# Attention and out-projection in one program per layer: a two-layer gated cross-attention kernel on one core

## What is computed

```
x = x + tanh(g_xattn[0]) * attn0(layernorm(x), ctx)   # 32 heads, 8 kv heads, 128 features, q and k rms-normed
x = x + tanh(g_ffn[0])   * scaled_ffn(layernorm(x))
x = x + tanh(g_xattn[1]) * attn1(layernorm(x), ctx)   # 16 heads, 4 kv heads, 96 features
x = x + tanh(g_ffn[1])   * routed_lora(layernorm(x))

attn(latents, context):                # 8 batches, 112 latent rows, 375 context rows, 1024 features
    kv = concat(context, latents)      # 487 rows
    q, k, v = latents @ Wq, kv @ Wk, kv @ Wv
    out = softmax(q k^T * scale) v     # 4 heads share one kv head
    return out @ Wo
```

## Time and profile before

| | us |
|---|---|
| median of 3 runs | 3026.83 (3024.57 to 3027.17) |
| span of the profiled execution | 3023.0 |
| PE busy, share | 2842.8, 94% |
| PEld busy, share | 2421.8, 80% |
| ACT busy, share | 1214.6, 40% |
| DVE busy, share | 1164.5, 39% |
| POOL busy, share | 710.5, 24% |

### The profile page before, as it was taken

The page is one execution under the profiler, slowest core; times in us unless marked ns, Lnnn a source line. Parts: engine busy times, 40 slices in busy tenths (PEclk is TensorE's granted clock), DMA queues, the critical chain, the costliest instruction groups (busy, mean ns, idle before and its releaser), DMA issues. The chain is left out here.

```text
span 3023.0 us, 43041 instructions
## 1 busy us (share of the span) xinstructions
PE 2842.8 (94%) x14487; PEld 2421.8 (80%) x14487; DVE 1164.5 (39%) x2034; ACT 1214.6 (40%) x2550; POOL 710.5 (24%) x585
## 2 busy tenths in 40 slices
PE   6999999799999997999998999598998998998997
PEld 5888887688888886888886888477998997887885
DVE  4333330411112116777772332643101112776335
ACT  4333332322222216777772323434322223785223
POOL 1111110300000005666655732120000001553400
PEclk9999999899999998999998999798998999999998
DMA  4233333222221213333336721102241222332312
GB/s 143 77 101 101 100 102 112 100 63 68 67 61 61 62 55 110 106 106 106 107 88 158 179 65 55 66 1 79 82 117 56 92 92 79 81 83 71 87 34 63
DMA packets 331149, 259.89 MB, mean 86 GB/s; under 512 B 190160, under 2 KB 285768, under 8 KB 331056
## 3 DMA queue, kind: packets, MB, share of 16 engines
q1 hardware_dynamic: 331056, 258.63, 29.3%
HBM read 190.66 MB, written 67.91 MB: 86 GB/s over the span
## 5 line engine op out<-in xcount | busy, mean ns | idle before, releaser
L42 PE MATMUL kv_y<-kv_whi,kv_xthi 128*125 128x512 f32 (+1 forms) x1152 | 446.0, 387 | 4.6 <-DVE kv_wlo L295 4.2
L44 PE MATMUL kv_y<-kv_whi,kv_xtlo 128*125 128x512 f32 (+1 forms) x1152 | 434.7, 377 | 0.0
L43 PE MATMUL kv_y<-kv_wlo,kv_xthi 128*125 128x512 f32 (+1 forms) x1152 | 433.9, 377 | 0.0
L42 PE MATMUL q_y<-q_whi,xthi 128*128 128x512 f32 (+1 forms) x1008 | 386.3, 383 | 8.0 <-ACT q_qn L487 4.7
L44 PE MATMUL q_y<-q_whi,xtlo 128*128 128x512 f32 (+1 forms) x1008 | 376.7, 374 | 0.0
L43 PE MATMUL q_y<-q_wlo,xthi 128*128 128x512 f32 (+1 forms) x1008 | 376.2, 373 | 0.0
L1000 DVE TENSOR_TENSOR at_ptlo<-at_tb,at_pthi 125x448 fp32r<-125x448 f32 (+1 forms) x384 | 238.2, 620 | 143.8 <-ACT at_pthi L953 137.9
L42 PE MATMUL o_y<-o_whi,o_ohi 128*128 128x512 f32 (+1 forms) x672 | 267.3, 398 | 14.4 <-DVE o_olo L1163 12.1
L953 ACT ACTIVATE at_pthi<-at_tb 125x448 fp32r<-125x448 f32 (+1 forms) x384 | 210.1, 547 | 136.2 <-PE at_tb L909 131.9
L43 PE MATMUL o_y<-o_wlo,o_ohi 128*128 128x512 f32 (+1 forms) x672 | 263.9, 393 | 0.0
L44 PE MATMUL o_y<-o_whi,o_olo 128*128 128x512 f32 (+1 forms) x672 | 263.8, 393 | 0.0
(11 more groups left out here) (192 smaller groups left out, 4819.9 us busy)
## 6 DMA issues: line engine op xcount, KB each, us to landing
kv_xin<-in_ctx_dram SPq DMA_DIRECT2D x48, 500.0 KB
q_raw<-in_L_xattn_Wq_dram SPq DMA_DIRECT2D x8, 2048.0 KB, 8.5
o_raw<-in_L_xattn_Wo_dram SPq DMA_DIRECT2D x64, 256.0 KB, 2.6
qT_d<-q_stage SPq DMA_DIRECT2D x56, 256.0 KB, 2.6
at_qr<-qT_d SPq DMA_DIRECT2D x64, 224.0 KB, 3.2
o_rb<-rT_d SPq DMA_DIRECT2D x32, 448.0 KB
v_d<-kv_stage SPq DMA_DIRECT2D x48, 250.0 KB
kT_d<-kv_stage SPq DMA_DIRECT2D x48, 250.0 KB, 4.5
```

What stands on the lines that cost most here:

```text
L42: pe.matmul(out, stat_hi, mov_hi, start=start, stop=False)
L43: pe.matmul(out, stat_hi, mov_lo, start=False, stop=False)
L44: return pe.matmul(out, stat_lo, mov_hi, start=False, stop=stop)
```

## The change

`attention`, `out_project` and the old `attend` are replaced by one `attend`. It is straight-line code: Python loops over all units, no hardware loop.

- Units now run kv head by kv head (a group g of 8 batches; `u = g * 8 + b`), and the projection of group g-1 is woven into the units of group g. A piece is one row tile of 128 tokens by 512 columns over the 4 heads of a group: 4 blocks of 128 features in layer 0 (12 matmuls), 3 in layer 1 (9 matmuls). There are 14 per group; a unit has an early piece (behind T1, not in batch 0) and a late one (behind V1, not in batch 7). All pieces use one PSUM bank `y`, and DVE adds each to the residual (`add`) before the next begins. The last group's 14 pieces come at the end, over four banks. The scores have three banks in place of four.
- The row sums' reciprocals are stored and fetched per unit: `spread_sums(u)` writes the 112 x 4 tile transposed to DRAM (runs of one element), `fetch_sums(u)` reads it back for all partitions. On SP both stand in one queue with the loads: sums of u stored, q, k, v of u+2 loaded, a slab of Wo loaded, sums of u fetched. `load(u+2)` has the same five DMAs as before.
- DVE normalizes each unit out of PSUM (`take_o`); ACT and POOL cut it into `oh` and `ol`. `oT` is gone.
- In layer 1 the four heads of 96 features are packed into three blocks of 128: block j holds head j and 32 features of head 3. Wo's slabs are loaded in the same order by two DMAs, turned on PE into `y`, and cut by ACT and DVE. 24 slabs take the place of 32; in layer 0 there are 64 as before, cut by ACT and POOL.
- The rows of x for the residual are loaded at the start of the stage.

```diff
@@ -96,7 +96,7 @@
-                      dram(f"rT{n}_d", (BATCH, L.heads, QLEN)))
+                      dram(f"rT{n}_d", (L.units, G, QLEN)))
...
+        def attend(n, L, x_sb, wo, source=None):
...
+            D, U, NB = L.d, L.units, BATCH
...
+            flip = not L.normed
+            NG = L.kvh
+            NK = G * D // P
+            NS = 2 * NK
...
+            def slab_step(m):
+                half, j = m // NK, m % NK
+                return half * 4 + j if not flip else m if half == 0 else 4 + j
...
+            def early_of(u):
+                g, k = u // NB, u % NB
+                return PIECES * (g - 1) + 2 * k - 1 if g and k else None
+            def late_of(u):
+                g, k = u // NB, u % NB
+                return PIECES * (g - 1) + 2 * k if g and k < NB - 1 else None
...
+            def piece(q):
+                g, i = q // PIECES, q % PIECES
+                if g < NG - 1:
+                    return g, i // TT, i % TT
+                return g, i % 2, i // 2
...
+                rb = sb(st, f"{tag}_rb", [D, 2, G, QLEN])
+                on = sb(st, f"{tag}_on", [P, 2, NK, QLEN]) if flip else rb
+                oh = sb(st, f"{tag}_oh", [P, 2, NK, TOKENS], F32R)
...
+                raw = sb(st, f"{tag}_raw", [P, RAW, BANK])
+                w_hi = sb(st, f"{tag}_whi", [P, 3, NK, BANK], F32R)
...
+                s = [ps(st, f"{tag}_s{i}", [P, BANK]) for i in range(3)]
...
+                y = ps(st, f"{tag}_y", [P, BANK])
+                tail_banks = [y] + s
...
+                        def load(u):
+                            g, b, p = u // NB, u % NB, u % 2
+                            if u >= 2:
+                                sp.wait_ge(q_cut, u - 1)
+                                sp.wait_ge(k_cut, u - 1)
+                            sp.dma_start(qr[:, p, :].rearrange("d (g s) -> d g s", g=G),
+                                         qT_d[g, :, :, b * QLEN:(b + 1) * QLEN]).then_inc(qk_loaded[p], 16)
+                            sp.dma_start(kr[:, p, 0:CTX], kT_d[b * L.kvh + g, :, :]).then_inc(qk_loaded[p], 16)
+                            sp.dma_start(kr[:, p, CTX:KVLEN], kl_d[g, :, b * QLEN:(b + 1) * QLEN]).then_inc(qk_loaded[p], 16)
+                            if u >= 2:
+                                sp.wait_ge(v_cut, u - 1)
...
+                            sp.dma_start(vr[0:CR, p, 0:CT, :], v_d[b * CTX:(b + 1) * CTX, cols].rearrange("(j r) d -> r j d", r=CR)).then_inc(v_loaded[p], 16)
+                            sp.dma_start(vr[0:QLEN, p, CT, :], vl_d[b * QLEN:(b + 1) * QLEN, cols]).then_inc(v_loaded[p], 16)
...
+                        def spread_sums(u):
+                            sp.wait_ge(inverted, u + 1)
+                            sp.dma_start(rT_d[u].rearrange("h s -> s h"), rinv[:, u % 2, :], allow_slow_non_contiguous=True).then_inc(r_stored[u % 2], 16)
+                        def fetch_sums(u):
+                            sp.wait_ge(r_stored[u % 2], 16 * (u // 2) + 16)
+                            if u >= 2:
+                                sp.wait_ge(o_taken if flip else o_lo, u - 1)
+                            sp.dma_start(rb[:, u % 2, :, :], rT_d[u:u + 1].broadcast_to([D, G, QLEN])).then_inc(r_loaded[u % 2], 16)
...
+                        load(0)
+                        load(1)
+                        if source is not None:
+                            for t in range(TT):
+                                sp.dma_start(x_sb[:, t, :], source[t * P:(t + 1) * P, :]).then_inc(x_loaded, 16)
...
+                        for w in range(RAW):
+                            load_slab(w)
...
+                        for u in range(U):
+                            spread_sums(u)
+                            if u + 2 < U:
+                                load(u + 2)
+                            if u % NB in SLAB_AT and slabs < NG * NS:
+                                load_slab(slabs)
...
+                            fetch_sums(u)
...
+                        def cut_o(u):
+                            g, b, p = u // NB, u % NB, u % 2
...
+                            pool.wait_ge(o_hi, u + 1)
+                            pool.tensor_tensor(ol[:, g % 2, :, cols], on[:, p, :, :], f32(oh[:, g % 2, :, cols]), ALU.subtract).then_inc(o_lo, 1)
...
+                        def project_piece(q, bank):
+                            g, half, t = piece(q)
+                            i = 2 * g + half
+                            pe.wait_ge(w_lo_s, NK * (i + 1))
+                            pe.wait_ge(o_lo, units_for(g, t))
+                            for k in range(NK):
+                                last = product(pe, bank[:], oh[:, g % 2, k, t * P:(t + 1) * P], ol[:, g % 2, k, t * P:(t + 1) * P],
+                                               w_hi[:, i % 3, k, :], w_lo[:, i % 3, k, :], k == 0, k == NK - 1)
+                            last.then_inc(projected, 1)
+                        def project_early(u):
+                            q = early_of(u)
+                            if q is not None:
+                                pe.wait_ge(added, q)
+                                if flip:
+                                    pe.wait_ge(w_lo_s, slabs_by(u))
+                                project_piece(q, y)
+                        def project_late(u):
+                            q = late_of(u)
+                            if q is not None:
+                                if q:
+                                    pe.wait_ge(added, q)
+                                if flip:
+                                    pe.wait_ge(w_lo_s, slabs_by(u + 1))
+                                project_piece(q, y)
+                        def turn_slab(u):
+                            if flip and u % NB in SLAB_AT:
+                                w = slabs_by(u)
+                                done = pieces_by(u) + (early_of(u) is not None)
+                                if done:
+                                    pe.wait_ge(added, done)
+                                if w:
+                                    pe.wait_ge(w_lo_s, w)
+                                pe.wait_ge(raw_loaded[w % RAW], 32 * (w // RAW) + 32)
+                                for m in range(G):
+                                    last = pe.transpose(y[:, m * P:(m + 1) * P], raw[:, w % RAW, m * P:(m + 1) * P], ident[:])
+                                last.then_inc(w_turned, 1)
...
+                            scores(0, h)
+                        for u in range(U):
+                            more = u + 1 < U
+                            if more:
+                                scores(u + 1, 0)
+                            turn(u, 0)
+                            if more:
+                                scores(u + 1, 1)
+                            turn(u, 1)
+                            project_early(u)
+                            if more:
+                                scores(u + 1, 2)
+                            if u:
+                                multiply(u - 1, 2)
+                            turn(u, 2)
+                            turn_slab(u)
+                            if more:
+                                scores(u + 1, 3)
+                            if u:
+                                multiply(u - 1, 3)
+                            multiply(u, 0)
+                            turn(u, 3)
+                            multiply(u, 1)
+                            project_late(u)
+                        multiply(U - 1, 2)
+                        multiply(U - 1, 3)
+                        first = PIECES * (NG - 1)
+                        for i in range(PIECES):
+                            pe.wait_ge(added, max(first, first + i - 3))
+                            project_piece(first + i, tail_banks[i % 4])
...
+                        def cut_o(u):
+                            g, b, p = u // NB, u % NB, u % 2
+                            act.wait_ge(o_taken, u + 1)
+                            if g >= 2 and b == 0:
+                                act.wait_ge(projected, PIECES * (g - 1))
+                            act.activation(oh[:, g % 2, :, b * QLEN:(b + 1) * QLEN], on[:, p, :, :], ACT.Copy).then_inc(o_hi, 1)
...
+                            high(u, 0)
+                            if u + 2 < U:
+                                cut_q(u + 2)
+                            high(u, 1)
+                            if more:
+                                exp(u + 1, 0)
+                                exp(u + 1, 1)
+                            high(u, 2)
+                            if u % NB in SLAB_AT:
+                                cut_slab(slabs_by(u))
+                            if more:
+                                exp(u + 1, 2)
+                            if u:
+                                cut_o(u - 1)
+                            high(u, 3)
+                            if more:
+                                exp(u + 1, 3)
```

(71 more changed lines are left out.)

489 lines of the change are left out of this document (158 added, 331 removed).

## The result

| | before | after |
|---|---|---|
| median of the runs, us | 3026.8 | 4163.8 (4152.6 to 4171.2, 4 runs) |
| ratio after / before, 95% interval | | 1.3756 (1.3734 to 1.3778) |
| span of the profiled run, us | 3023.0 | 4169.4 |
| PE busy, us | 2842.8 | 3047.5 |
| layer 0, first score to end of last add | 1150.7 to 1915.6 | 1145.8 to 2766.9 |

The changed kernel is 37.6% slower. I had forecast 8% slower, 3268 us, with a range up to 3461. The sign was right; the size was not, and the time lies far above the range. Layer 0 ends 851 us later (forecast 161), and layer 1 adds 295 (forecast 80).

The account below looks back on a forecast made before the run. The prediction took TensorE's own pace to bound the kernel, with a load wait of 5.4 us added per unit. Span 3023 + 161 (layer 0) + 80 (layer 1) = 3264, plus 3.8 for the median: 3268 us, range 3110 to 3461.

Parts of the forecast that it names:

- The place: SP's queue: load(u+2) stands behind the store of u's sums, so its full latency falls between two DVE instructions.
- the 8.75 us chain: Layer 0 unit with both pieces: from the load's landing through cuts, PE work, late piece and add to the next reciprocal, 8.75 us.
- the 12.24 worked out: PE's own work in a layer 0 unit with two pieces: 6.80 + 24 x 0.2267 = 12.24 us.
- the store at nothing: The 4-byte row-sum store ahead of the loads: nothing added for the middle, up to 2 us for the upper bound.
- L: Load latency between DVE's reciprocal and cut_k, in all but two units per layer: 5.4 us, range 3.7 to 7.5.
- Rival (c): The 4-byte store holds the queue longer, each run 0.2 us or more: L of 9 us, 3600 us; chance 0.07.
- The clock: PE's clock falls to half in each unit's gap: +230 us in 70 units with a late piece, 3500 us; chance 0.10.
- The savings: Two stage boundaries, about 30 us, and layer 1's packing, 38 us: 68 us earlier if PE stays the pace.
- The prediction's 2955: Whole kernel if PE stays the pace: ends at 2955 us; with the load hidden, 2959, a rival with chance 0.06.
- chain of 7.0 us for a unit without pieces: First 8 units of layer 0, without pieces: the chain over DVE and ACT ends by 7.0 us, against 6.80 of PE work.
- the 38 us of the packing: Layer 1's projection: packing 16 heads into 12 blocks cuts 672 matmuls to 504, 168 x 0.2267 = 38 us saved.
- the 30 of the boundaries: PE's loss between attention and projection, 13.4 + 2.5 us in layer 0 and 11.6 + 2.5 in layer 1, about 30 saved.

Follow-up runs that it names:

- experiment 1: Changed kernel with the store of the row sums left out, the fetch reading x instead (sums not applied): 3429.5 us.
- experiment 9: Changed kernel with 16-byte store runs, q and k loaded one unit further ahead, the slab's load one unit later: 3009.2 us, 0.9948 of the kernel before.
- experiment 4: Changed kernel with the same 448 4-byte runs each written 512 bytes from the next, the fetch reading x (sums not applied): 3434.6 us.
- experiments 3: Changed kernel storing the sums of two of four heads, 224 runs of 4 bytes, the fetch reading x (sums not applied): 4066.2 us.

## Why the prediction was wrong in size and right in kind

**The place, the chain, the sign: right.** In the kernel after, the reciprocal, the store, the load and the cuts follow each other as described, and the 8.75 us chain was measured at 8.78 to 8.80 in all 14 units of experiment 1 in which the granted clock stayed at 1.00. With the loads moved out of it, PE took over the pace: a steady unit with two pieces in experiment 9 is 12.3 us, against the 12.24 worked out.

**The term that failed: the store at nothing.** I took L = 0.25 + 0.45 + 4.7 and for the 4-byte store up to 2 us more, by the store of the earlier trace rows. That row was the nearest by kind but not by what counts: its runs are 448 bytes long, so no two of its writes come near each other except at their ends. Here 112 writes lie in each 448 bytes. The store lands after 10.3 us at the median, and L is 13.4 us. Without the store it is 6.2, so the store is 7.2 us of L, and 666 us over the 92 units. Experiment 1 against the kernel after gives 734, the clock's share with it. The step from "no row so short" to "small runs as such need not cost much" was true (experiment 4) and yet no bound for this store. Rival (c) had the sign, loads that land after 6 us and more (11.1 here), and a price of 0.2 us a run, which experiments 3 and 4 refute. Its total, L of 9, was still too small, and 0.07 too little chance for a kind of transfer that no row showed.

The prediction set a rule of the Trainium skill beside this (DMA: Bandwidth & Descriptors, Specifications: below 512 bytes a transfer is a read-modify-write). By size alone, wherever the writes lie, the kernel of experiment 4 should have been as slow, and it was not; the measurement decides. That a load needs longer when a slow store is in front of it agrees with another section of the Trainium skill (DMA: Bandwidth & Descriptors, Queues, rings and completion order), by which the receipt of a transfer lands only after all earlier writes of the same DMA engine: 11.1 us for the kl load here, 3.1 in experiment 4.

**The rest of L: one value for two layers.** Without the store L is 7.2 us in layer 0 and 4.0 in layer 1, where the sum had 5.4 for both: 73 us too little over the 92 units. The earlier trace rows had shown 5.87 and 3.80 from the q load's issue to the cut; I took 4.7, and experiment 1 has 5.4 and 3.9. The wake and the store's issue were put at 0.7. In layer 0 the head of the queue takes 1.85 in experiment 1, with no store to issue: the slab's load, waiting for POOL, and the fetch stand in front of the next unit's q load, 2.7 us in the unit shown. I had listed what waits behind the new wait on DVE, ACT and PE, and for SP only the store.

**The clock: a rival that came on top.** I gave 0.10 to a fall in every gap, as a case of its own at L = 5.4. It isn't one of its own: it comes with L. In the kernel after, the gaps are about 10 us and T2 to the late piece takes 6.25 instead of 3.34, 2.9 us in the unit shown; its chain from 1713.89 to 1725.49 is 11.60. The whole excess can be added up from the trace. Over the 92 units the waits sum to 1236 us where 92 x 5.4 = 497 had been forecast, 739 more. The chains sum to 959 us where the prediction's add up to 788, 171 more. The two make 910, and the span is 905 us above the forecast 3264. Of the 171, 102 are in the 48 units of layer 0 with a late piece: 10.92 us each, against 8.79 at a clock of 1.00. The other 69 are in the units without one and in layer 1, where the clock was not told from other causes. In experiment 1 the same sums are 73 and 99. So the store costs 666 us by itself and 72 more through longer chains. The cases of my range were added one at a time, while the first of them brings the second with it.

**The savings: real, but smaller than 68 us.** The prediction's 2955 for a kernel at PE's pace is tested by experiment 9, where DVE waits for a load six times, 46.5 us in all, 43.3 of it before the first unit of each layer. It has a span of 3007.7. Layer 0's last add ends there at 1917.7 (before 1915.6), layer 1's at 2937.0 (2953.4): 16 us, not 68. In layer 0 the eight units without pieces take 69.4 us by the distances of their reciprocals where 8 x 6.80 = 54.4 had been assumed (7.9 in six of them, 10.2 in one, 11.6 the first). Each later group of eight takes 94.1 where 8 x 6.80 + 14 x 2.72 = 92.5 is PE's work. In layer 1 the first eight take 82.5, 28 more than the same 54.4. My own chain of 7.0 us for a unit without pieces had said that PE is not the pace there; the sum of savings left it out. How the 38 us of the packing and the 30 of the boundaries divide in what was gained was not measured apart.

## What to carry to other kernels

When a step is inserted in a queue, follow the queue in both directions: what stands behind the new transfer and is needed at once, and which waits ahead of it now hold that. If the trace has no store of the form that a change adds, compare not only the size of its runs but how near they lie to each other, and keep the upper bound wide. Where the rows show two values for one term, one for each layer, carry both through the sum. A wait that grows can bring a second cost with it: behind the gaps of some 10 us TensorE came back here at half its clock (0.50 from 1715 to 1721). Such terms belong in one case and not in two rivals.

## What the runs showed of the hardware that I had not expected

- Writes of 4 bytes side by side: a store of 448 of them lands after 10.3 us at the median. At a distance of 16 bytes it is 4.3, at 64 bytes 3.6, at 512 bytes 3.4. With half as many side by side it is still 8.9. One run of 16 bytes per partition lands after 3.4 us.
- Issues of transfers can block: SP was held for 7.59 us in a single issue, where the usual one is 0.3 to 0.9 us. In the two attention stages of the kernel after, 26 issues took over 2 us. Without the store (experiment 1) there were four, the longest 4.1 us, so the slow store makes this frequent but is not alone in it.
- The clock's answer to a gap is not given by its length alone: behind 2.42 us of idle PE it stayed at 1.00 in one unit and fell in another (0.76 over 7 us); behind 4.38 us it read 0.57 over the next 7 us. A chain of one and the same work took 8.8 us at 1.00, 10.2 to 10.4 at 0.83 or 0.84, and 10.7 to 11.8 at 0.66 to 0.73.
